# Gated cross-attention block on one core: attention of the third and fourth sequence by gathered rows, picks by marked sets, and a new set-up order

## What is computed

```python
q = layernorm(x) @ W_q.T + b_q
scores = q @ desc_router.T / sqrt(256)            # [8, 256, 64]
scores = where(set in token_to_sets[token], scores, -inf)
w = softmax(top 2 of scores, -inf elsewhere)
x = x + tanh(g_xattn) * (w @ ctx)                 # ctx: [8, 64, 256]
xt = layernorm(x)
gate, up = xt @ Wg.T, xt @ Wu.T                   # Wg, Wu [2048, 256], dequantised
inter = gelu_tanh(gate) * up
x = x + tanh(g_ffn) * (inter @ Wd.T)              # Wd [256, 2048], dequantised
```

## Time and profile before

| | us |
|---|---|
| median of 3 runs (310.4 to 311.25) | 310.67 |
| the profiled execution, time | 311.26 |
| its span | 309.5 |
| TensorE busy | 302.0 |
| VectorE busy | 223.6 |
| ScalarE busy | 155.9 |
| GpSimd busy | 144.8 |

### The profile page before, as it was taken

The page is one execution under the profiler, slowest core; times in us unless marked ns, Lnnn a source line. Parts: engine busy times, 40 slices in busy tenths (PEclk is TensorE's granted clock), DMA queues, the critical chain, the costliest instruction groups (busy, mean ns, idle before and its releaser), DMA issues.

```text
span 309.5 us, 4648 instructions
## 1 busy us (share of the span) xinstructions
PE 302.0 (98%) x1537; PEld 251.0 (81%) x1537; DVE 223.6 (72%) x478; ACT 155.9 (50%) x287; POOL 144.8 (47%) x138
## 2 busy tenths in 40 slices
PE   6998999999999999999999999999999999999996
PEld 4777888787788788888888888888888888888885
DVE  3999999899985669687676678777676565544545
ACT  3476665657455453435555453444654533444341
POOL 3447455636742342876353325866442233432421
PEclk9999999999999999999999999999999999999999
DMA  6970440020000021326240111424130001110102
GB/s 184 253 186 0 150 124 0 0 37 1 0 2 0 2 34 17 77 57 123 70 101 3 17 17 26 94 53 85 63 94 0 0 15 26 26 40 0 37 0 68
DMA packets 47288, 16.11 MB, mean 52 GB/s; under 512 B 38944, under 2 KB 44448, under 8 KB 47264
## 3 DMA queue, kind: packets, MB, share of 16 engines
q1 hardware_dynamic: 44576, 12.92, 18.0%
q0 software_dynamic: 864, 2.10, 2.5%
q10 hardware_dynamic: 1824, 0.79, 1.1%
HBM read 11.08 MB, written 3.15 MB: 46 GB/s over the span
## 4 chain that ended last, share of the span: by engine, by line
PE 78%; issue 7%; POOL 6%; DVE 4%; ACT 2%; DMA 2%; SPq 0%; DVEq 0%; POOLq 0%
PE ring_ps L1317 49%; PE acc_ps L1351 17%; PE acc_ps L1364 4%; PE att_ps L1364 3%; POOL act_lo L525 3%; POOL w_nat L507 2%; DMA x_sb<-in_x_dram 2%; PE att_ps L1219 1%; POOL w_nat L518 1%; PE ring_ps L1302 1%; ACT act L695 1%; DVE act L1006 0%; DVE act L1000 0%; DVE x_sb L1157 0%; ACT act L691 0%
## 5 line engine op out<-in xcount | busy, mean ns | idle before, releaser
L525 POOL TENSOR_TENSOR act_lo<-act,act_hi 128x512 fp32r<-128x512 f32 x63 | 82.1, 1302 | 118.8 <-ACT act_hi L702 118.6
L1317 PE MATMUL ring_ps<-xt_hi,w_hi 128*128 128x512 f32 (+1 forms) x264 | 103.8, 394 | 1.0 <-ACT xt_hi L675 0.7
L1317 PE MATMUL ring_ps<-xt_hi,w_lo 128*128 128x512 f32 (+1 forms) x264 | 100.9, 384 | 0.0
L1317 PE MATMUL ring_ps<-xt_lo,w_hi 128*128 128x512 f32 (+1 forms) x264 | 100.2, 384 | 0.0
L691 ACT ACTIVATE act<-ring_ps 128x512 f32<-128x512 f32 x64 | 38.1, 596 | 84.2 <-PE ring_ps L1317 83.8
L1000 DVE SCALAR_TENSOR_TENSOR act<-act,ring_ps 128x512 f32<-128x512 f32 x64 | 43.7, 683 | 39.1 <-ACT act L691 38.9
L1006 DVE SCALAR_TENSOR_TENSOR act<-act,ring_ps 128x512 f32<-128x512 f32 x64 | 43.8, 685 | 27.2 <-ACT act L695 25.9
L1317 PEld LDWEIGHTS ring_ps<-xt_hi,w_hi 128*128 128x128 f32 x264 | 49.7, 188 | 11.1 <-issue 1.2
L1317 PEld LDWEIGHTS ring_ps<-xt_lo,w_hi 128*128 128x128 f32 x264 | 49.0, 188 | 10.3 <-DVE xt_lo L938 0.2
L695 ACT ACTIVATE act<-act 128x512 f32<-128x512 f32 x64 | 40.5, 632 | 32.7 <-DVE act L1000 32.7
L1317 PEld LDWEIGHTS ring_ps<-xt_hi,w_lo 128*128 128x128 f32 x264 | 49.8, 188 | 8.3
(11 more groups left out here) (129 smaller groups left out, 331.9 us busy)
## 6 DMA issues: line engine op xcount, KB each, us to landing
x_t<-in_x_dram SPq DMA_DIRECT2D x48, 32.0 KB, 2.1
w_nat<-w_nat SPq DMA_DIRECT2D x96, 16.0 KB
out_dram<-x_sb SPq DMA_DIRECT2D x6, 256.0 KB, 2.2
x_sb<-in_x_dram SPq DMA_DIRECT2D x1, 1024.0 KB, 8.4
ln_dram<-normed SPq DMA_DIRECT2D x16, 64.0 KB, 2.2
w_nat<-ln_dram SPq DMA_DIRECT2D x16, 64.0 KB, 2.0
packed<-L_ffn_gate_W_packed_dram SPq DMA_DIRECT2D x3, 256.0 KB, 2.9
packed<-n_L_ffn_up_W_packed_dram SPq DMA_DIRECT2D x3, 256.0 KB, 3.3
```

The lines of the kernel that those rows point to most:

```text
L525: pool.tensor_tensor(act_lo[:, s % RING, :], act[:, s % ACT_RING, :], act_hi[:, s % RING, :].bitcast(F32), ALU.subtract).then_inc(inter_lo, 1)
L1317: i = pe.matmul(into[:, tok], wt[:, n, w], xt[:, c % 2, k, tok], start=(k, j) == order[0], stop=(k, j) == order[-1])
```

## The change

- `BY_ROWS` falls from 4 to 2: sequences 2 and 3 are attended by gathered rows too, in chunk 0. Their WEIGH and ATTEND come a step earlier for sequence 2, ADD a step later for sequence 3. The load of their context rows into SBUF is gone.
- The bias is loaded as a 65th row of the router tile (one row of 256), transposed with it, and its product with the router is two matmuls. The multiply and sum on VectorE are gone. The token indices are loaded from ScalarE's queue instead of GpSimd's.
- Sequences 0 and 1 no longer look up indices. The two best values stay in `top8`, its six other places and six spare columns of `scores` get a constant, `match_replace` writes a mark where a score is one of the eight, ScalarE makes one weight per set (two tanh over 64 sets and one addition of 1), and one VectorE instruction multiplies mark and weight. The scores are halved for this.
- The opening's lists are written in a new order on every engine; `score(2)` moves from step 2 into it.

```diff
-    SCORE_SCALE = float(D) ** -0.5
+    SCORE_SCALE = 0.5 * float(D) ** -0.5
-    FIRST_STEPS = ((None, None, 2, 3, 5, 6, 7, 9, 10, 10), (7, 8, 8, 9, 10, 11, 12, 14, 15, 15))
+    FIRST_STEPS = ((None, None, 2, 3, 4, 5, 7, 9, 10, 10), (7, 8, 8, 9, 10, 11, 13, 14, 15, 15))
-    BY_ROWS = 2 * CB
+    BY_ROWS = CB
...
-            sp.dma_start(router_sb[:, :], router).then_inc(router_loaded, 16)
+            sp.dma_start(router_sb[0:SETS, :], router).then_inc(router_loaded, 16)
-            load_ctx(CB, BY_ROWS, ctx_rest_loaded)
...
-            sc.dma_start(bq_sb[:, :], b_q.rearrange("(a d) -> a d", a=1).to_broadcast([SETS, D])).then_inc(small_loaded, 16)
+            sc.dma_start(router_sb[SETS:SETS + 1, :], b_q.rearrange("(a d) -> a d", a=1)).then_inc(small_loaded, 16)
+            sc.dma_start(tok_sb[:, :, :], token_sets.rearrange("(p h) k -> p h k", h=HALVES)).then_inc(tokens_loaded, 16)
...
+                for h in range(HALVES):
+                    i = sc.activation(soft[:, q, h, :], scores[:, q, h, 0:SETS], ACT.Tanh, bias=lead[:, q, h:h + 1], scale=2.0)
+                sc.activation(soft[:, q, :, :], soft[:, q, :, :], ACT.Identity, bias=1.0).then_inc(lead_tanh_ready, 1)
...
+                dve.scalar_tensor_tensor(lead[:, q, :], top8[:, q, :, 0], -1.0, top8[:, q, :, 1],
+                                         ALU.mult, ALU.subtract).then_inc(lead_ready, 1)
+                mark(("spares", b), dve.memset(top8[:, q, :, 2:8], SPARE))
...
-                mark(("picked", b), dve.tensor_tensor(
-                    picked[:, q], iota_i[:, :].unsqueeze(1).unsqueeze(1).to_broadcast([P, HALVES, 2, SETS]),
-                    top8_at[:, q, :, 0:2].unsqueeze(3).to_broadcast([P, HALVES, 2, SETS]), ALU.is_equal))
+                for h in range(HALVES):
+                    i = dve.match_replace(marked[:, h, :], top8[:, q, h, :], scores[:, q, h, :], CHOSEN)
...
+                dve.scalar_tensor_tensor(probs[:, q, :, :], marked[:, :, 0:SETS], CHOSEN, soft[:, q, :, :],
+                                         ALU.is_equal, ALU.mult).then_inc(probs_ready, 1)
...
+            score(CB)
```

More of the change, by code:

```diff
@@ L18 @@
 LN_EPS = 1e-5
-MASKED = -3.0e38
+MASKED = -1.0e38
+CHOSEN = 2.0e38
+SPARE = 3.0e38
 GELU_CUBIC = 0.044715
@@ L472, in _ @@
             pool.memset(minus_half[:, :], -0.5).then_inc(minus_half_made, 1)
+            pool.memset(scores[:, :, :, SETS:], SPARE).then_inc(spares_made, 1)
             for i, g in enumerate((g_xattn, g_ffn)):
@@ L557, in _ @@
             root_2(1)
-            for i in range(2):
-                scale_rows_of(1, i)
+            scale_rows_of(1, 0)
+            scale_rows_of(1, 1)
+            root_1(CB)
             scale_down_of(1)
-            root_1(CB)
-            for i in range(2):
-                scale_rows_of(2, i)
+            scale_rows_of(2, 0)
+            scale_rows_of(2, 1)
             for c in range(CHUNKS):
@@ L862, in find_where @@
                     return
-                mark(("picked", b), dve.tensor_tensor(
-                    picked[:, q], iota_i[:, :].unsqueeze(1).unsqueeze(1).to_broadcast([P, HALVES, 2, SETS]),
-                    top8_at[:, q, :, 0:2].unsqueeze(3).to_broadcast([P, HALVES, 2, SETS]), ALU.is_equal))
+                if b == 0:
+                    dve.wait_ge(spares_made, 1)
+                after(("spares", b))
+                for h in range(HALVES):
+                    i = dve.match_replace(marked[:, h, :], top8[:, q, h, :], scores[:, q, h, :], CHOSEN)
+                mark(("marked", b), i)
             def weigh(b):
@@ L1064, in _ @@
             update_variance(1)
-            rows_low(1)
+            input_variance(CB)
             find_shift(1)
+            unpack(1, 1)
             unpack(1, 2)
+            unpack(2, 0)
+            unpack(2, 1)
+            ln2_low(1)
             down_tile_low(0)
             turn_blocks(CB)
-            input_stats(CB)
-            ln2_low(1)
-            input_variance(CB)
-            for stage in range(3):
-                unpack(2, stage)
             cubic(0)
@@ L1319, in project, with first_products, second_products @@
                 return i
+            def first_products(kind, u):
+                if kind == "gate":
+                    pe.wait_ge(rows_lo, u + 1)
+                bank_free(kind, u)
+                project(0, u, ("gate", "up").index(kind), bank_of(kind, u), slice(0, ST), 1)
+            def second_products(kind, u, done):
+                project(0, u, ("gate", "up").index(kind), bank_of(kind, u), slice(ST, TOK), 2).then_inc(done, 1)
             def gate(s):
@@ L1450, in _ @@
                     for b in next_sequences(c, n, SCORE):
-                        score(b)
+                        if b > CB:
+                            score(b)
                     for b in next_sequences(c, n, ATTEND):
```

154 lines of the change are left out of this document (76 added, 78 removed).

## The result

The changed kernel takes 313.92 us (median of 4, 313.42 to 314.97) where the kernel before takes 310.53 us (median of 4, 310.36 to 311.25): the ratio is 1.0106, 95% interval 1.0085 to 1.0127. It is **slower by 1.1%**, outside the forecast range. Its profiled execution took 313.42 us at a span of 311.6 us, 2.1 us more than the profiled span of before.

The account below looks back on a forecast made before the run. TensorE was taken to set the pace, with VectorE binding too in chunk 0. The terms -1.6 + 0 + 1.4 gave -0.2 us, from 310.67 to a median of 310.5 us; range 308.5 to 312.0 us.

Parts of the forecast that it names:

- What bounds the kernel: TensorE sets the pace from the first product, VectorE binding with it in chunk 0; later chunks stay untouched.
- Term 1: Opening, up to unit 2's cubic: 1.6 us less, from the bias wait 0.4, the picks 1.4, re-ordering 0.2 against.
- The picks' price: Choosing sets for sequences 0 and 1 on VectorE: 0.95 us against 1.65 each, 1.4 us less in all.
- Term 2: Sequence 2, units 4 to 10: no change; TensorE's 0.85 us saved are given back through GpSimd's gathers and VectorE's additions.
- the four additions cost 1.67 us: Sequence 2 on VectorE: four additions at 1.67 us replace one 0.69 us instruction; 0.5 us more in all.
- Term 3: Sequence 3, units 10 to 16: late rows delay root, shift and normalisation, so `gate(16)` starts 1.4 us later.
- both waits named: TensorE at units 14 and 15: new waits on the normalised copy and the gating, 1.5 to 2 us together.
- The slower rival on the gathers: GpSimd, units 11 and 12: gathers held by VectorE instructions, two of them giving +1.2 us, 311.9 us; 15%.
- The rival on the opening: Opening set by landings and hand-overs, not VectorE's work: only 0.4 us gained, +1.0 us, 311.7 us; 9%.

Follow-up runs that it names:

- e1: The changed kernel with sequences 2 and 3 attended by one-hot and matmul as before, so the new opening alone; ratio 1.0050 to the kernel before.
- e9: e1 with TensorE's list up to the first attention, warm-up counts included, put back as in the kernel before; ratio 1.0040.
- e10: e9 with the token numbers loaded first on GpSimd's queue, as in the kernel before; ratio 1.0027.
- e0: The changed kernel measured again, nothing altered; ratio 1.0104 to the kernel before.
- e2: The kernel before with sequences 2 and 3 attended by gathered rows and its opening kept, less their context load; ratio 1.0098.
- e3: e2 with GpSimd made to wait for sequence 2's variance before scaling, so it is idle during the four additions; one execution, 314.95 us.
- e4: e2 with sequence 3's shift behind the cubic of unit 14 and its normalisation behind that unit's square; ratio 1.0078.
- e7: e2 with the four additions of sequence 2 left out, its rows still gathered; one execution, 310.40 us.
- e5: The kernel before with 12 instead of 15 warm-up matmuls ahead of the router's transposes; ratio 1.0023.
- e11: e10 with seven tiny memsets of an unused tile on VectorE ahead of its first wait; ratio 0.9997.
- e8: e2 with the rows of sequences 2 and 3 brought by eight plain loads of fixed rows instead of GpSimd's gathers; one execution, 311.18 us.
- e6: The changed kernel with 15 instead of 12 warm-up matmuls ahead of the router's transposes; ratio 1.0095.
- e12: The changed kernel with TensorE's list up to the first attention, warm-up counts and token load place as in the kernel before; ratio 1.0093.

## Why the prediction was wrong

**What bounds the kernel**: right. In the changed kernel everything was decided in chunk 0, and the shift at `gate(16)`, 2.20 us, is the whole difference of the profiled pair. "Nothing that the change moves reaches them", of the later chunks, does not hold in general: the new opening without the rows loses 1.2 to 1.4 us in chunk 2 (e1, e9, e10).

**Term 1, the opening, forecast -1.6.** Mis-sized, and the step that failed is "x was there 0.4 us before VectorE took it, with the bias as 65th row this wait is gone". The picks' price was right (in e0 two matches from 12.83 to 13.32 us, product 0.29, memset 0.07), but the head waited for the token numbers instead (2.02 us), a moved DMA whose landing I did not cost, though I had listed the bias's: the statistics start 0.21 us later and not 0.4 earlier, which is 0.6 of the 0.8 us that were missing. In the profile the term is -0.84, and the old opening alone reaches -0.48 to -1.15 (e2, e3, e4, e7), so a gain is not shown by it. And three warm-up matmuls fewer, which I set at nothing, put TensorE at half speed in some executions (e5; the changed kernel's own in e0), by up to 3.3 us at unit 2. With both put back (e10) the opening is 0.5 to 1.2 us ahead of the old one in its profile, and e11's ratio leaves at most 0.4 us of that in the time.

**Term 2, sequence 2, forecast 0.** TensorE's 0.85 us came (1.64 ahead at 59.10 us, of which 0.84 was there at unit 2), and the gathers took what I read from chunk 1 (1.09 and 0.97 us). The rows landed by 59.6 us, not at 61.0, and TensorE's instructions waited 0.3 us at most for the scaling behind the gathers. The step that failed is "the four additions cost 1.67 us": I took their price from a stretch in which GpSimd was silent, and put them beside its scaling. They took 4.01 us instead, and the held one is worth 2.35 us at unit 8 (e2 against e3), hence +1.7 where 0 stood.

**Term 3, sequence 3, forecast +1.4.** Right: both waits named came (0.66 and 0.76 us), root, shift and normalisation queued as written, and from unit 8 to unit 16 the kernel lost 1.3 us (+0.87 to +2.20). The last gather landed after the product of unit 13, but by 0.3 us only (product to 93.20 us, first addition at 93.53), and with rows that are there in time most of the loss stays (e8).

**Sum and rivals.** -0.8 + 1.7 + 1.3 = +2.2 instead of -0.2 in the profiled pair. The slower rival on the gathers named the right two engines and the wrong one as held: VectorE's additions were held, not the gathers (none over 1.09 us). The rule of the Trainium skill that it leans on is about descriptors; the one that bears on what happened is about reads (cited at e3). The rival on the opening named landings and was nearer than my term.

**Open**: what VectorE's rest of 0.46 us is; why GpSimd's queued instructions went ahead of a waiting addition; what the 0.5 us of the medians beyond the rows are; and how far TensorE's half speed depends on the warm-up's count, the pause behind it or chance.

## What to carry to other kernels

Price an instruction by a row of the same neighbourhood, not only of the same shape: in this kernel a VectorE instruction with two operands in SBUF cost what it costs alone plus what GpSimd had in hand, so check what GpSimd does in the stretch that it is moved to. When an opening is re-ordered, warm-up matmuls and small loads are terms of the sum too, and one profile can miss a cost that comes in five executions of twelve; the spread of the spans shows it.

## What the runs showed that I had not expected

- **An addition held over three instructions.** Alone it takes 0.47 us; beside two scalings and an `act_lo` of GpSimd it took 2.78 to 2.89 us (the changed kernel, e0, e2, e4, e6, e12), beside one `act_lo` 1.52 us (e10). It goes the other way too: where the additions came first, `act_lo` took 1.62 us instead of 1.29 (before, 214.98 us).
- **The same collision in chunk 2.** In e3 to e6 and e12 one addition of sequence 7 met an `act_lo` (1.51 us in e5, 1.55 in e12, 0.48 in e2): 1 us at unit 42, of which 0.2 stay. A shift of tenths decides it.
- **TensorE's half speed is not in the granted clock.** It reads 1.00 from 8 to 10 us in e0, where 11 matmuls fill 2 us (19 in the kernel before); the lengths of like matmuls show it.
- **A rest of VectorE at a fixed count.** With semaphore waits counted, the rests in e1, e9 and e10 stand 128 records of VectorE apart; in the changed kernel, whose list is eight longer, the one rest stands at the same number as the second of e10, but two units earlier (293.57 us, unit 60). Seven instructions more moved both out of sight (e11). At the number of the first the changed kernel's VectorE waits 0.81 us for ScalarE anyway, which would hide a rest. Against a fixed count stands that the kernel before shows a rest at neither number, though its VectorE runs on there without a gap that could hide one. The Trainium skill, Runtime: NRT & Kernel Launch, Instruction fetch mechanics, has an engine's instructions come in blocks of 256 and the crossing mostly hidden; the spacing here is half of that, and one rest cost 1.3 us by what it pushed. That fetching is the cause was not shown.
